# Splitting a projection in two, moving a weighting step and handing a copy from GpSimd to VectorE in a double attention kernel

## Chip, cores and metric

One Trainium2 chip, one core. The metric is the device time of one launch in microseconds (us). The engines are TensorE (PE; its weight loads are shown as PEld), VectorE (DVE), ScalarE (ACT), GpSimd (POOL) and the DMA queues, of which SyncE (SP) issues nearly all.

## What is computed

The layer takes x of 32 batches, 512 tokens and 256 channels, and puts two attentions and one routed feed-forward network behind each other. The feed-forward part is added to batch 0 alone (512 routed rows).

```python
qk = x @ W_attn + b_attn; q, k = qk[..., :C], qk[..., C:]     # 16 heads of 16 channels
y  = causal_attn(q, k, v=x)
e  = x[:, 1:] - y[:, :-1]
k2 = x[:, :-1] @ W_k2 + b_k2
y2 = causal_attn(q[:, 1:], k2, e)
x1 = layernorm(x + proj(y) + proj(y2))        # then layernorm(x1 + ffn(x1))
```

## The kernel before

The work of attention is cut into **units**: one unit is four heads of one attention of one batch, so a batch has 8 units, at **places** 0 to 7 (0 to 3 the first attention, 4 to 7 the second), and the kernel has 256. A unit has ten **slots**. Every engine walks through the same list of times (unit, slot), and does in each slot what is written for it there; within an engine the order is fixed by hand. Semaphores are the only thing that joins the engines. `ahead` is the batch of the present unit.

In each slot TensorE makes one PSUM bank of transposed scores for the present unit (`score_t`, three banks, L682) and one bank of plain scores for the unit five ahead (`score`, three banks, L693), the two next to each other in the upper and lower rows of the array. ScalarE turns each `score_t` bank into probabilities by Exp (L541), GpSimd sets the upper triangle of each pair of banks to zero (L437, slots 1, 3, 5, 7, 9), VectorE takes the row maxima of the `score` banks (L899). The maxima are needed by the unit five ahead: at places 3 and 7, slots 2 and 3, they are transposed (L747), negated and split (L575, L908), and four DMAs of SyncE put them into rows of `stack_q` (L374).

TensorE groups its banks: 0, 1, 2 in slot 0; 3, 4 in slot 3; 5, 6, 7 in slot 5; 8, 9 in slot 8 (`RUNS`). Between them stand, in this order:

- slot 2: `weigh` of the unit before, key blocks 1, 3 and 2 (24 matmuls, L643), which needs all five masks of that unit. ScalarE copies the result to `heads_t` (L567, its slot 2).
- slot 4: the four transposes of `heads_t` (L708). VectorE normalises out of `out_t` behind its own bank 4 (L922, L928).
- slot 7: a **piece** of the projections of the next batch (`PIECES`), six matmuls of 512 columns into the one bank `misc` (L734), at places 7, 0, 1, 2, 4 and 5; at places 3 and 6 instead half of the output projection of the batch before (L776, 8 matmuls for two token blocks j = 0, 1).
- slot 9: `weigh` of the present unit, key block 0 (8 matmuls, L643), which needs the masks of slots 1 and 3 (banks 0 to 3), and VectorE's normalisation of the unit before.

ScalarE reads a piece out of `misc` in slot 7, behind Exp 7 (`part_f`, L553). GpSimd splits it into two parts three slots later, that is in slot 0 of the next unit (`part_h` L457, `part_l` L459), and SyncE issues six DMAs to the stacks in slot 4 (L295).

At places 0 and 1 ScalarE also applies the layer norm of an earlier batch, one quarter each in slots (0,7), (0,9), (1,1) and (1,3) (L276), behind a chain of small operations of GpSimd (`refine`, slot (0,5)) that ends in `shift` (L264). GpSimd adds the bias to `resid` at (3,6) (L445), splits x for the next projections at (6,4) and (6,7) (L469, L471), copies x into `value1` at (5,2) (L483), and in every slot 0 does one 128x256 subtraction or addition (L496, L503).

Of the kernel before, what the change touches and what calls it, by code (L numbers as in the profile page):

```python
# [11 lines left out]
ALU = mybir.AluOpType  # L12
# [3 lines left out]
HEADS, HEAD_DIM = 16, 16  # L16
GROUP = 4
GROUPS = HEADS // GROUP
UNITS = 2 * GROUPS
# [26 lines left out]
TRIANGLES = [(512, 2, 1), (512, 2, 1), (512, 2, 2), (512, 2, 2), (256, 4, 1)]  # L46


PIECES = {(7, 7): ("k", 0, 0), (0, 7): ("q", 0, 1), (1, 7): ("k", 1, 2), (2, 7): ("q", 1, 3),
          (4, 7): ("k2", 0, 4), (5, 7): ("k2", 1, 5)}  # L50
N_PIECES = len(PIECES)
RING, KEY_DEPTH, MAX_DEPTH, JUNK = 6, 3, 3, 2

# [16 lines left out]
def build_layer(nc, x, x_turned, w_attn, b_qk, w_k2, w_proj, b_proj,  # L70
                router_indices, routing_weights, w_up, b_up, w_down, b_down, out):
    batches, tokens, width = x.shape
    blocks = tokens // P
    halves = width // P
# [11 lines left out]
    with ctx:  # L86
# [232 lines left out]
        def _(e):  # L319
# [5 lines left out]
            for time in times:  # L325
# [28 lines left out]
                    e.dma_start(resid[:, :, :], x[b].rearrange("(t p) c -> p t c", p=P)).then_inc(s_resid, 16)  # L354


                ended = time - 7
                piece = piece_ending(ended // SLOTS % UNITS, ended % SLOTS, ended // SLOTS // UNITS, batches)
                if piece and not (piece[0] == "q" and piece[2] == 0):
                    stack_piece(e, *piece)  # L360
# [48 lines left out]
        def _(e):  # L409
# [17 lines left out]
            for time in times:  # L427
# [9 lines left out]
                    e.affine_select(out=view, in_=view, compare_op=ALU.is_ge, fill=0.0, base=-unit_parts(unit)[1],  # L437
                                    pattern=[[0, runs], [0, cut], [1, P]], channel_multiplier=-1).then_inc(s_mask, 1)

                if (place, slot) == (3, 6) and 0 <= ahead - 1 < batches:  # L440
                    wide = bass.AP(bias2[:, :].tensor, bias2[:, :].offset, [list(bias2[:, :].ap[0]), [0, blocks], [1, width]])
                    if ahead == 1:
                        e.wait_ge(s_bias, 1)
                    e.wait_ge(s_resid, 16 * ahead)
                    e.tensor_tensor(resid[:, :, :], resid[:, :, :], wide, ALU.add).then_inc(s_biased, 1)  # L445
# [16 lines left out]
                for c in range(halves):  # L462
                    b = ahead + 2
                    if (place, slot) == (6, (4, 7)[c]) and 0 <= b < batches:
                        if c == 0:
                            e.wait_ge(s_xt, 16 * (b + 1))
                            if b:
# [2 lines left out]
                        e.wait_ge(s_xsplit, 2 * (halves * b + c) + 1)  # L470
                        e.tensor_tensor(x_t[LOW][:, c, :], x_full[:, c, :], x_t[HIGH][:, c, :].bitcast(F32),  # L471
                                        ALU.subtract).then_inc(s_xsplit, 1)


                if (place, slot) == (5, 2) and 0 <= ahead + 1 < batches:
                    b = ahead + 1
                    if b == 0:
                        e.wait_ge(s_wproj, 32)
                        e.tensor_tensor(bias2[:, :], bias2[:, :], bias2[:, :], ALU.add).then_inc(s_bias, 1)
                    e.wait_ge(s_x, 16 * (b + 1))  # L480
                    if b:
                        e.wait_ge(s_pv, GROUP * (UNITS * (b - 1) + GROUPS))
                    e.tensor_copy(value1[:, :, :, 0:HEAD_DIM],  # L483
                                  x_in[:, :, :].rearrange("p t (h d) -> p t h d", d=HEAD_DIM)).then_inc(s_value1, 1)


                done = unit - 2
# [37 lines left out]
        def _(e):  # L525
# [4 lines left out]
            for time in times:  # L530
# [21 lines left out]
                        e.wait_ge(s_split, 2 * (n - 1))  # L552
                    e.activation(part_f[n % 2][:, :], misc[:, :], ACT.Identity, bias=bias_qk[:, column:column + 1]).then_inc(s_full, 1)  # L553

                ended = time - 7
                piece = piece_ending(ended // SLOTS % UNITS, ended % SLOTS, ended // SLOTS // UNITS, batches)
                if piece and piece[0] == "q" and piece[2] == 0:
                    stack_piece(e, *piece)
# [70 lines left out]
        def _(e):  # L629
# [17 lines left out]
            for time in times:  # L647
# [61 lines left out]
                    done.then_inc(s_turned, 1)  # L709


                piece = piece_ending(place, slot, ahead, batches)
                if piece:
                    kind, hf, b, n = piece
                    if n == 0:
                        e.wait_ge(s_wsplit, 2)
                    if kind == "k2" and b == 0:
                        e.wait_ge(s_wsplit, 4)
                    if n:
                        e.wait_ge(s_full, n)  # L720
                    if place == 1 and ahead >= 1:
                        e.wait_ge(s_yt, halves * ahead - 1)
                    if place == 2 and ahead >= 1:
                        e.wait_ge(s_yt, halves * ahead)
                    if place == 4 and ahead >= 1:
                        e.wait_ge(s_attended, 2 * ahead - 1)
                    if place == 7 and ahead + 1 >= 0:
                        e.wait_ge(s_negl, 2 * ahead + 3)
                    for c in range(halves):
                        if n % N_PIECES == 0:  # L730
                            e.wait_ge(s_xsplit, 2 * (halves * b + c + 1))
                        for i, (pw, px) in enumerate(zip(PARTS_K, PARTS_Q)):
                            w = wk2[pw][:, c, hf, :] if kind == "k2" else wq[pw][:, c, hf + (0 if kind == "q" else halves), :]
                            done = e.matmul(misc[:, :], w, x_t[px][:, c, :], start=(c == 0 and i == 0),  # L734
                                            stop=(c == halves - 1 and i == TERMS - 1))
                    done.then_inc(s_piece, 1)
# [14 lines left out]
                if 0 <= b < batches:  # L751
                    for hf in range(halves):
                        if (place, slot) == ((1, 4), (2, 4))[hf]:
                            e.wait_ge(s_full, min(N_PIECES * (b + 2) + 2 + hf, N_PIECES * batches))
                            if hf == 0:
                                e.wait_ge(s_added, GROUPS * (b + 1))
                            else:
                                e.wait_ge(s_yt, halves * b + 1)
                            for t in range(blocks):
                                done = e.transpose(misc[:, t * P:(t + 1) * P], y_sum[b % 2][:, t, hf * P:(hf + 1) * P], ident[:, :])  # L760
                            done.then_inc(s_yt_pe, 1)
                    for pair in range(2):
                        for j in range(2):
                            if (place, slot) == ((3, 6)[pair], 7):
                                t = 2 * pair + j
                                if j == 0:
                                    if b == 0:
                                        e.wait_ge(s_wproj, 32)
                                    e.wait_ge(s_yt, halves * (b + 1))
                                    e.wait_ge(s_full, min(N_PIECES * (b + 2) + (6 if pair else 4), N_PIECES * batches))  # L770
                                    if pair:
                                        e.wait_ge(s_attended, 2 * b + 1)
                                    elif ahead < batches:
                                        e.wait_ge(s_negl, 2 * ahead + 2)
                                for c in range(halves):
                                    done = e.matmul(misc[:, j * width:(j + 1) * width], y_t[:, c, t * P:(t + 1) * P], wp[:, c, :],  # L776
                                                    start=(c == 0), stop=(c == halves - 1))
                                if j:
                                    done.then_inc(s_proj, 1)


                if slot == 9 and 0 <= unit < end:
                    b, a, g = unit_parts(unit)
                    if a:
                        e.wait_ge(s_value2, GROUPS * b + g + 1)
# [70 lines left out]
        def _(e):  # L856
# [27 lines left out]
            for time in times:  # L884
# [3 lines left out]
                if 0 <= unit + LEAD < end:  # L888
                    b, a, g = unit_parts(unit + LEAD)
                    number = time + SLOTS * LEAD  # L890
                    for i, (h, qb, col) in enumerate(MAX_BANKS[slot]):
# [5 lines left out]
                        if count >= JUNK:  # L897
                            e.wait_ge(s_max, count - JUNK + 1)
                        e.tensor_tensor_reduce(junk[count % JUNK][:, 0:n], score[number % MAX_DEPTH][:, col:col + n], mask, 1.0, -3e38,  # L899
                                               ALU.add, ALU.max, max_cols[b % 2][:, a, head % SIDES, head // SIDES, qb:qb + 1]).then_inc(s_max, 1)  # L900

                for a, b in ((0, ahead + 1), (1, ahead)):
                    if (place, slot) == ((7, 3), (3, 3))[a] and 0 <= b < batches:
# [142 lines left out]
```

## Time and profile before

| | |
|---|---|
| runs | 2417.51, 2409.24, 2413.22 us; median 2413.22 |
| profiled execution | 2417.51 us, its span 2415.4 us |
| TensorE busy in the span | 2319.0 us, 96% |
| VectorE busy | 2089.4 us, 87% |
| ScalarE busy | 1778.4 us, 74% |
| GpSimd busy | 1523.3 us, 63% |

The span is the time from the first to the last recorded instruction. The busy time of TensorE has modelled ends, so it also holds short stretches in which the array waits behind the last columns of a matmul; starts of instructions are the better measure there.

### The profile page before, as it was taken

Reading aid. Unit: us, or ns where it says so; the run is one execution under the profiler, and the core shown is the slowest. Engines: PE = TensorE matmul, PEld = TensorE weight load, DVE = VectorE, ACT = ScalarE, POOL = GpSimd, SP = SyncE. Lnnn points to the kernel's source line nnn. Section 1 sums busy time; section 2 is a strip of 40 time slices with the busy share of each in tenths; the row PEclk is TensorE's granted clock in tenths of the full one; section 3 lists DMA queues with packets and bytes.
Section 4 is the critical chain, followed back from the end, with each engine's and each line's share of the span. In section 5 each row is a group of like instructions: output and inputs, shape, how many; then the busy total and the mean of one; then the engine's idle time right before and its main releaser. Section 6 shows DMA issues by size and latency. Waiting matters only on the chain.

```text
span 2415.4 us, 64954 instructions
## 1 busy us (share of the span) xinstructions
PE 2319.0 (96%) x19670; PEld 1327.7 (55%) x19670; DVE 2089.4 (87%) x9242; ACT 1778.4 (74%) x3392; POOL 1523.3 (63%) x2375
## 2 busy tenths in 40 slices
PE   6999999999999999999999999999999999999996
PEld 4555555555555555555555555555555555555454
DVE  5889998899899989999899889999998899998554
ACT  3677777777777777777777777777777777777642
POOL 4466666766766666666666666666666667665432
PEclk7799999999999999999999999999999999999997
DMA  7465555655556556565555665655556555554121
GB/s 122 90 109 105 103 99 98 118 113 112 115 104 112 97 103 123 111 114 112 103 107 101 108 118 111 118 111 108 104 95 117 112 113 117 110 97 81 55 70 35
DMA packets 187732, 250.82 MB, mean 104 GB/s; under 512 B 26744, under 2 KB 103168, under 8 KB 187392
## 3 DMA queue, kind: packets, MB, share of 16 engines
q1 hardware_dynamic: 186432, 245.10, 53.6%
q8 instruction: 166, 2.72, 0.5%
q10 hardware_dynamic: 960, 1.57, 0.5%
q14 instruction: 174, 1.43, 0.3%
HBM read 74.60 MB, written 16.78 MB: 38 GB/s over the span
## 4 chain that ended last, share of the span: by engine, by line
PE 72%; ACT 12%; issue 6%; POOL 4%; DVE 3%; DMA 2%; SPq 1%; ACTq 0%; DVEq 0%; POOLq 0%
PE out_t L643 22%; PE score_t L682 18%; PE misc L734 11%; PE score L693 7%; ACT heads_t L567 5%; PE out_t L708 4%; PE misc L776 4%; ACT prob L541 4%; PE score L835 2%; DVE junk L899 2%; DMA stack_q<-neg_l 1%; POOL prob L437 1%; ACT resid L276 1%; PE misc L760 1%; SPq L374 1%
## 5 line engine op out<-in xcount | busy, mean ns | idle before, releaser
L899 DVE CUSTOM_DVE_ANT_0 junk<-score,mask_rows 128x384 bf16<-128x384 f32 (+3 forms) x3584 | 1686.6, 515 | 224.8 <-PE score L693 215.8
L541 ACT ACTIVATE prob<-score_t 128x512 f32<-128x512 f32 x2560 | 1368.4, 599 | 276.4 <-PE score_t L682 275.5
L437 POOL TENSOR_SCALAR_AFFINE_SELECT prob<-prob 128x512 f32<-128x512 f32 (+1 forms) x1280 | 710.5, 560 | 729.7 <-ACT prob L541 717.9
L682 PE MATMUL score_t<-stack_q,stack_k 50*128 50x128 f32 (+5 forms) x4096 | 985.2, 359 | 25.8 <-ACT prob L541 7.5
L693 PE MATMUL score<-stack_k,stack_q 48*128 48x512 f32 (+3 forms) x4096 | 982.5, 348 | 2.7 <-DVE max_cols L899 1.1
L682 PEld LDWEIGHTS score_t<-stack_q,stack_k 50*128 50x128 f32 (+1 forms) x4096 | 611.8, 186 | 565.6 <-ACT prob L541 304.1
L643 PE MATMUL out_t<-prob,value 128*17 128x512 f32 (+3 forms) x8192 | 658.0, 439 | 0.0
L693 PEld LDWEIGHTS score<-stack_k,stack_q 48*128 48x128 f32 x4096 | 618.4, 188 | 24.8 <-DVE max_cols L899 9.9
L899 DVE DVE_READ_ACCUMULATOR2_ANT max_cols<- 128x1 f32 x4096 | 339.5, 83 | 0.0
L643 PEld LDWEIGHTS out_t<-prob,value 128*17 128x17 f32 x8192 | 184.7, 97 | 211.1 <-issue 129.6
L459 POOL TENSOR_TENSOR part_l<-part_f,part_h 128x512 fp32r<-128x512 f32 x192 | 245.4, 1278 | 16.3
L567 ACT ACTIVATE heads_t<-out_t,sum_floor 128x512 f32<-128x512 f32 x256 | 176.7, 690 | 90.5 <-PE out_t L643 90.3
L553 ACT ACTIVATE part_f<-misc,bias_qk 128x512 f32<-128x512 f32 x192 | 132.2, 689 | 142.1 <-PE misc L734 142.1
L708 PE MATMUL out_t<-ident,heads_t 128*128 128x128 f32 x1024 | 167.8, 286 | 25.5 <-ACT heads_t L567 11.6
L708 PEld LDWEIGHTS out_t<-ident,heads_t 128*128 128x128 f32 x1024 | 107.6, 141 | 87.1 <-ACT heads_t L567 86.8
L899 DVE CUSTOM_DVE_ANT_0 junk<-score,mask_first 128x128 bf16<-128x128 f32 x512 | 146.2, 286 | 0.0
L457 POOL CAST part_h<-part_f 128x512 fp32r<-128x512 f32 x192 | 117.5, 612 | 44.0 <-ACT part_f L553 41.7
L734 PE MATMUL misc<-x_t_h,wq_h 128*128 128x512 f32 x256 | 118.1, 461 | 17.7 <-DVE wq_l L873 9.8
L776 PE MATMUL misc<-wp,y_t 128*128 128x256 f32 x512 | 128.3, 394 | 0.0
L776 PEld LDWEIGHTS misc<-wp,y_t 128*128 128x128 f32 x512 | 93.3, 191 | 21.1 <-issue 8.9
L734 PE MATMUL misc<-x_t_l,wq_h 128*128 128x512 f32 x256 | 103.7, 405 | 0.0
L734 PE MATMUL misc<-x_t_h,wq_l 128*128 128x512 f32 x256 | 103.7, 405 | 0.0
(99 smaller groups left out, 1703.0 us busy)
## 6 DMA issues: line engine op xcount, KB each, us to landing
stack_k<-part_h SPq DMA_DIRECT2D x512, 128.0 KB, 4.5
stack_k<-part_l SPq DMA_DIRECT2D x256, 128.0 KB, 5.1
stack_q<-part_h SPq DMA_DIRECT2D x248, 128.0 KB, 4.2
x_full<-x_turned SPq DMA_DIRECT2D x32, 512.0 KB, 13.1
x_in<-L_attn_x SPq DMA_DIRECT2D x32, 512.0 KB, 14.5
resid<-L_attn_x SPq DMA_DIRECT2D x32, 512.0 KB, 5.2
stack_q<-part_l SPq DMA_DIRECT2D x124, 128.0 KB, 5.1
layer_out<-resid SPq DMA_DIRECT2D x31, 512.0 KB, 7.6
```

The costliest lines, as they stand in the source:

```text
L437: e.affine_select(out=view, in_=view, compare_op=ALU.is_ge, fill=0.0, base=-unit_parts(unit)[1], pattern=[[0, runs], [0, cut], [1, P]], ch ...
L459: e.tensor_tensor(part_l[i][:, :], part_f[i][:, :], part_h[i][:, :].bitcast(F32), ALU.subtract).then_inc(s_split, 1)
L541: e.activation(prob[pair % RING][:, slot % 2 * 512:slot % 2 * 512 + 512], score_t[time % KEY_DEPTH][:, :], ACT.Exp, scale=1.0 / np.sqrt(HE ...
L553: e.activation(part_f[n % 2][:, :], misc[:, :], ACT.Identity, bias=bias_qk[:, column:column + 1]).then_inc(s_full, 1)
L567: e.activation(heads_t[:, :], out_t[:, :], ACT.Identity, bias=sum_floor[:, 0:1]).then_inc(s_heads, 1)
L643: done = e.matmul(out_t[32 * h:32 * h + HEAD_DIM + 1, first:first + count], value[:, kb, GROUP * g + h, :], prob[pair % RING][:, at:at + c ...
L682: done = e.matmul(score_t[now % KEY_DEPTH][:, col:col + n], keys[rows, pair, kb * P:(kb + 1) * P], stack_q[b % 2][rows, pair, kb * P:token ...
L693: done = e.matmul(score[number % MAX_DEPTH][:, col:col + n], stack_q[b % 2][rows, pair, qb * P:(qb + 1) * P], keys[rows, pair, 0:n], start ...
L708: done = e.transpose(out_t[:, t * P:(t + 1) * P], heads_t[:, t * P:(t + 1) * P], ident[:, :])
L734: done = e.matmul(misc[:, :], w, x_t[px][:, c, :], start=(c == 0 and i == 0), stop=(c == halves - 1 and i == TERMS - 1))
L776: done = e.matmul(misc[:, j * width:(j + 1) * width], y_t[:, c, t * P:(t + 1) * P], wp[:, c, :], start=(c == 0), stop=(c == halves - 1))
L899: e.tensor_tensor_reduce(junk[count % JUNK][:, 0:n], score[number % MAX_DEPTH][:, col:col + n], mask, 1.0, -3e38, ALU.add, ALU.max, max_co ...
```

## The change

It touches five things.

1. A piece is cut in two: the three matmuls of channel half c = 0 stay in slot 7, those of c = 1 go to slot 9. The piece now ends in slot 9, so that `part_f` is read in ScalarE's slot 9 (behind Exp 9), and GpSimd splits it in slot 2 of the next unit. SyncE's DMAs stay in slot 4 of the next unit.
2. The output projection at places 3 and 6 is cut in two as well: block j = 0 in slot 7, j = 1 in slot 9.
3. `weigh` of key block 0 goes from slot 9 to slot 7, behind the first half of a piece or of the projection and ahead of banks 8 and 9.
4. The copy of x into `value1` at (5,2) goes from GpSimd to VectorE, behind its maxima of bank 2.
5. The addition of the bias to `resid` on GpSimd goes from (3,6) to (3,2), where it stands ahead of the split of the piece of place 2.

```diff
-PIECES = {(7, 7): ("k", 0, 0), (0, 7): ("q", 0, 1), (1, 7): ("k", 1, 2), (2, 7): ("q", 1, 3),
-          (4, 7): ("k2", 0, 4), (5, 7): ("k2", 1, 5)}
+PIECES = {(7, 9): ("k", 0, 0), (0, 9): ("q", 0, 1), (1, 9): ("k", 1, 2), (2, 9): ("q", 1, 3),
+          (4, 9): ("k2", 0, 4), (5, 9): ("k2", 1, 5)}
...
-                ended = time - 7
+                ended = time - 5
...
-                if (place, slot) == (3, 6) and 0 <= ahead - 1 < batches:
+                if (place, slot) == (3, 2) and 0 <= ahead - 1 < batches:
...
-                if (place, slot) == (5, 2) and 0 <= ahead + 1 < batches:     # on GpSimd
...
-                    e.tensor_copy(value1[:, :, :, 0:HEAD_DIM],
-                                  x_in[:, :, :].rearrange("p t (h d) -> p t h d", d=HEAD_DIM)).then_inc(s_value1, 1)
...
-                piece = piece_ending(place, slot, ahead, batches)
-                if piece:
+                for c in range(halves):
+                    piece = piece_ending(place, slot + 2 * (1 - c), ahead, batches)
+                    if piece:
...
-                            if (place, slot) == ((3, 6)[pair], 7):
+                            if (place, slot) == ((3, 6)[pair], (7, 9)[j]):
...
-                if slot == 9 and 0 <= unit < end:
+                if slot == 7 and 0 <= unit < end:
...
+                if (place, slot) == (5, 2) and 0 <= ahead + 1 < batches:     # on VectorE, behind its maxima
...
+                    e.tensor_copy(value1[:, :, :, 0:HEAD_DIM],
+                                  x_in[:, :, :].rearrange("p t (h d) -> p t h d", d=HEAD_DIM)).then_inc(s_value1, 1)
```

## Rows read from the trace of the kernel before

**Rows 1.** The page, part 1: span; busy time, share and instructions of each engine.

```profile
span 2415.4 us, 64954 instructions
PE 2319.0 (96%) x19670; PEld 1327.7 (55%) x19670; DVE 2089.4 (87%) x9242; ACT 1778.4 (74%) x3392; POOL 1523.3 (63%) x2375
```

**Rows 2.** Windows of units, key-block-0 weighting to weighting: length, busy PE, PEld, DVE, ACT, POOL.

```profile
1001.09:1010.02 8.93, 8.78 (x79) 5.14 (x77) 7.66 (x36) 6.12 (x14) 6.79 (x8) 1.00 0.81 149
...
1018.49:1026.71 8.22, 8.13 (x76) 4.70 (x74) 7.55 (x34) 6.52 (x14) 6.18 (x9) 1.00 0.50 89
...
1052.51:1062.04 9.53, 8.95 (x80) 5.09 (x78) 7.65 (x35) 8.68 (x18) 6.24 (x11) 1.00 0.90 160
...
sum 69.55, PE 68.02 PEld 39.08 DVE 62.95 ACT 53.94 POOL 46.55; mean PE 8.50 PEld 4.89 DVE 7.87 ACT 6.74 POOL 5.82
```

**Rows 3.** Timeline of TensorE, a unit at place 5: start us, length us, instruction.

```profile
1019.47 0.50 PE L682 MATMUL score_t<-stack_q,stack_k 52*128 52x512 f32 x1
...
1020.43 1.49 PE L643 MATMUL out_t<-prob,value 128*17 128x384 f32 x24
...
1022.73 0.66 PE L708 MATMUL out_t<-ident,heads_t 128*128 128x128 f32 x4
...
1024.40 0.50 PE L734 MATMUL misc<-x_t_h,wk_h 128*128 128x512 f32 x1
...
1025.66 0.40 PE L734 MATMUL misc<-x_t_l,wk_h 128*128 128x512 f32 x1
1025.99 0.38 PE L682 MATMUL score_t<-stack_q,stack_k 52*128 52x256 f32 x1
...
1026.71 1.05 PE L643 MATMUL out_t<-prob,value 128*17 128x512 f32 x8
1027.69 0.50 PE L682 MATMUL score_t<-stack_q,stack_k 52*128 52x512 f32 x1
```

**Rows 4.** Timeline of TensorE, a unit at place 3: bank 0, output projection, bank 8.

```profile
1002.08 0.50 PE L682 MATMUL score_t<-stack_q,stack_k 50*128 50x512 f32 x1
...
1007.43 1.99 PE L776 MATMUL misc<-wp,y_t 128*128 128x256 f32 x8
1009.35 0.38 PE L682 MATMUL score_t<-stack_q,stack_k 50*128 50x256 f32 x1
```

**Rows 5.** Timeline of GpSimd at place 3, and its copy at place 5.

```profile
1002.89 0.61 POOL L457 CAST part_h<-part_f 128x512 fp32r<-128x512 f32 x1
1003.58 1.27 POOL L459 TENSOR_TENSOR part_l<-part_f,part_h 128x512 fp32r<-128x512 f32 x1
...
1005.50 0.91 POOL L437 TENSOR_SCALAR_AFFINE_SELECT prob<-prob 128x256 f32<-128x256 f32 x2
...
1007.84 2.36 POOL L445 TENSOR_TENSOR resid<-resid,bias 128x1024 f32<-128x1024 f32 x1
...
1023.27 1.05 POOL L483 COPY value<-x_in 128x1024 f32<-128x1024 f32 x1
```

**Rows 6.** Timeline of ScalarE, places 0 and 1; in brackets the idle time before.

```profile
1051.95 0.69 ACT L553 ACTIVATE part_f<-misc,bias_qk 128x512 f32<-128x512 f32 x1 [0.24 <-PE misc L734]
1053.07 0.60 ACT L276 ACTIVATE resid<-resid,shift,rstd 128x256 f32<-128x256 f32 x1 [0.44 <-POOL shift L264]
1053.58 1.06 ACT L541 ACTIVATE prob<-score_t 128x512 f32<-128x512 f32 x2
```

**Rows 7.** Timeline of TensorE, place 1: the transposes of heads_t.

```profile
1057.71 0.66 PE L708 MATMUL out_t<-ident,heads_t 128*128 128x128 f32 x4 [0.37 <-ACT heads_t L567]
```

**Rows 8.** Timeline of VectorE, place 5: maxima of bank 2, bank 3 and the end of bank 4.

```profile
1021.27 0.69 DVE L899 CUSTOM_DVE_ANT_0 junk<-score,mask_rows 128x512 bf16<-128x512 f32 x1
...
1022.42 0.69 DVE L899 CUSTOM_DVE_ANT_0 junk<-score,mask_rows 128x512 bf16<-128x512 f32 x1 [0.45 <-PE score L693]
...
1023.72 0.08 DVE L899 DVE_READ_ACCUMULATOR2_ANT max_cols<- 128x1 f32 x1
```

**Rows 9.** All copies on VectorE of line 871: nanoseconds, start, shapes.

```profile
L871 DVE CAST wq_h<-wq_full x1: 979/979/979, 6.3 to 6.3; 128x1024 fp32r<-128x1024 f32 x1
```

More of the change, by code:

```diff
@@ L472, in _ @@
                                         ALU.subtract).then_inc(s_xsplit, 1)
-                if (place, slot) == (5, 2) and 0 <= ahead + 1 < batches:
[L476 to L482, printed above, removed]
-                    e.tensor_copy(value1[:, :, :, 0:HEAD_DIM],
-                                  x_in[:, :, :].rearrange("p t (h d) -> p t h d", d=HEAD_DIM)).then_inc(s_value1, 1)
                 done = unit - 2
@@ L553, in _ @@
                     e.activation(part_f[n % 2][:, :], misc[:, :], ACT.Identity, bias=bias_qk[:, column:column + 1]).then_inc(s_full, 1)
-                ended = time - 7
+                ended = time - 5
                 piece = piece_ending(ended // SLOTS % UNITS, ended % SLOTS, ended // SLOTS // UNITS, batches)
@@ L709, in _ @@
                     done.then_inc(s_turned, 1)
-                piece = piece_ending(place, slot, ahead, batches)
-                if piece:
[L714 to L729, printed above, removed]
+                for c in range(halves):
+                    piece = piece_ending(place, slot + 2 * (1 - c), ahead, batches)
+                    if piece:
+                        kind, hf, b, n = piece
+                        if c == 0:
+                            if n == 0:
+                                e.wait_ge(s_wsplit, 2)
+                            if kind == "k2" and b == 0:
+                                e.wait_ge(s_wsplit, 4)
+                            if n:
+                                e.wait_ge(s_full, n)
+                            if place == 1 and ahead >= 1:
+                                e.wait_ge(s_yt, halves * ahead - 1)
+                            if place == 2 and ahead >= 1:
+                                e.wait_ge(s_yt, halves * ahead)
+                            if place == 4 and ahead >= 1:
+                                e.wait_ge(s_attended, 2 * ahead - 1)
+                            if place == 7 and ahead + 1 >= 0:
+                                e.wait_ge(s_negl, 2 * ahead + 3)
                         if n % N_PIECES == 0:
@@ L735, in _ @@
                                             stop=(c == halves - 1 and i == TERMS - 1))
-                    done.then_inc(s_piece, 1)
+                        if c == halves - 1:
+                            done.then_inc(s_piece, 1)
                 for a, b in ((0, ahead + 1), (1, ahead)):
@@ L900, in _ @@
                                                ALU.add, ALU.max, max_cols[b % 2][:, a, head % SIDES, head // SIDES, qb:qb + 1]).then_inc(s_max, 1)
+                if (place, slot) == (5, 2) and 0 <= ahead + 1 < batches:
+                    b = ahead + 1
+                    if b == 0:
+                        e.wait_ge(s_wproj, 32)
+                        e.tensor_tensor(bias2[:, :], bias2[:, :], bias2[:, :], ALU.add).then_inc(s_bias, 1)
+                    e.wait_ge(s_x, 16 * (b + 1))
+                    if b:
+                        e.wait_ge(s_pv, GROUP * (UNITS * (b - 1) + GROUPS))
+                    e.tensor_copy(value1[:, :, :, 0:HEAD_DIM],
+                                  x_in[:, :, :].rearrange("p t (h d) -> p t h d", d=HEAD_DIM)).then_inc(s_value1, 1)
                 for a, b in ((0, ahead + 1), (1, ahead)):
```

## The prediction

> **What bounds the kernel now.** I read the busy shares first, then eight stretches of one batch, then the engines' timelines in them. TensorE is busy 96% of the span, VectorE 87%, ScalarE 74%, GpSimd 63% [rows 1]. The eight units of a batch take 69.55 us, in which TensorE is busy 68.02, VectorE 62.95, ScalarE 53.94 and GpSimd 46.55 [rows 2]; a unit at place 5 takes 8.22 us, one at place 1 9.53, and there ScalarE is busy 8.68 of it. So TensorE's queue is the path nearly everywhere, with two exceptions that matter here: the stretch of the layer norm at places 0 and 1, where ScalarE is the path (TensorE's transposes wait 0.37 us for `heads_t` [rows 7]), and places where VectorE works more than usual and holds back a bank.
>
> In the unit at place 5 the reader can take TensorE's order from the starts [rows 3]: bank 0 at 1019.47, `weigh` of blocks 1, 3, 2 from 1020.43, the transposes at 1022.73, the piece from 1024.40, bank 8 at 1025.99, `weigh` of block 0 at 1026.71, the next bank 0 at 1027.69. So a piece takes 1.59 us from its start to bank 8, banks 8 and 9 take 0.72, `weigh` of block 0 takes 0.98.
>
> **Item 1 to 3, TensorE.** Not one matmul is added or removed. What is added is a change of kind: before, slots 7 to 9 hold piece, banks 8 and 9, `weigh`; after, half a piece, `weigh`, banks 8 and 9, half a piece. That is one boundary more per unit, and the same at places 3 and 6 with the projection's blocks. What does a boundary cost? The piece spends 1.26 us from its first to its last start, five steps, so 0.25 each, but the steps inside are shorter than the first and the last: from the last start to bank 8 are 0.33 us [rows 3]. 512 columns at the granted full clock (the last but two columns of [rows 2] are 1.00, which is 2.4 GHz) are 0.213 us, six of them 1.28, so that a piece carries 0.31 us beyond its columns; `weigh` of block 0, four passes of 512 columns for four heads side by side (2048 columns, 0.85 us), carries 0.13. A small part of the 0.31 recurs with each matmul and does not come twice. I put the additional boundary between 0 (a half piece that runs into `weigh` without a gap) and 0.21 us, and take 0.10, nearer to the excess of `weigh`, since the new neighbours both use all rows of the array.
>
> The Trainium skill (TensorEngine Tiling (Array Packing), "Key Properties") says that changing the tiling mode, not merely the tile, drains TensorE. Scores use half the rows, pieces the whole array, `weigh` a column group per head, so by that page every boundary here costs a drain, the new one too. The trace agrees that a boundary has a price: 0.33 us between the last start of the piece and bank 8 where columns alone are 0.213. By the page the term below would be computed with 0.21 in place of 0.10 and be 37 us in place of 18.
>
> Of the eight boundaries of a batch I count 5.5: at place 0 it is hidden, because at place 1 ScalarE is late anyway; at place 5 it goes into the term of the copy; at place 7 VectorE works nearly without a gap and hides about half. 5.5 x 0.10 x 32 batches = **18 us**; from 0 to 5.5 x 0.21 x 32 = 37.
>
> In an ordinary unit the move of `part_f` is hidden. It is read when the second half ends, at bank 0 of the next unit, and takes about 0.6 us of ScalarE, while Exp 0 can't start before bank 0 is done anyway; the three Exps (0.53 each by the pair in [rows 6]) then end before `weigh` does, 2.4 us behind bank 0 (1020.43 plus 1.49 against 1019.47, [rows 3]), and `heads_t` starts when it did. If that cover were gone, 0.1 us a unit would be due.
>
> **ScalarE at places 0 and 1.** Before, ScalarE fills its wait for GpSimd's `shift` with `part_f` (0.69 at 1051.95), then still waits 0.44 us, and starts the first quarter of the norm at 1053.07 [rows 6]. From there on to `heads_t` it has no gap, and TensorE waits for it [rows 7]. After, slot 7 holds no `part_f`: ScalarE waits for `shift` with nothing to do, since its queue is in order, Exps 8 and 9 stand behind it, and `part_f` comes behind Exp 9, in the stretch without a gap. `shift` isn't earlier, for it hangs on the mask of bank 5 and on its own chain. So `heads_t` is late by about the 0.59 us of `part_f` that are not overlapped, and the transposes, banks 5 to 7 and the rest follow. I take 0.55 x 31 = **17 us**; between 0.3 (if TensorE's waits for ScalarE at place 1 have slack that I don't see) and 0.65, so 9 to 20.
>
> **Item 5, GpSimd at place 3.** Before, the split of the piece of place 2 starts at 1002.89, and lasts to 1004.85, ahead of the first mask of the unit; the masks of slots 1 and 3 follow at 1005.50, and the bias (2.36 us) at 1007.84, when nothing urgent is left [rows 5]. After, the order is: mask of slot 1, bias, split, mask of slot 3. With bank 0 as zero (1002.08 [rows 4]): `part_f` and two Exps end at 0.7 + 1.08 = 1.78, the mask (0.91 for two, so 0.42 to 0.45) at 2.2, the bias at 4.55, the split (0.61 + 1.27 and a gap, 1.96) at 6.5, the mask of slot 3 at 6.9. `weigh` of block 0 now stands in slot 7, behind the first half of the projection; the projection starts at 5.35 (at 1007.43, [rows 4]) and half of its 1.92 us to bank 8 (1009.35) puts `weigh` at 6.3. Its heads 2 and 3 need the mask of slot 3, so it stands 0.5 to 0.6 us. The other waits at TensorE grow shorter by it (VectorE catches up ahead of bank 8 and at place 4), so I count 0.35 x 31 = **11 us**; from 0 (the mask is in time) to 1.3 us, if heads 0 and 1 then run alone and the second pair takes the full 0.85 again, so 0 to 40. In the seven other units the mask of slot 3 is due at about 4.5 and `weigh` at 5.7, more than a microsecond of cover. The split moved behind the mask of slot 1 delays SyncE's six DMAs by about 2 us; the stacks are needed by the banks five units ahead, and at least a whole unit (8.2 us) lies between, so this costs nothing; without that cover each microsecond would stand on TensorE's path.
>
> **Item 4, the copy.** On GpSimd it takes 1.05 us [rows 5] in a unit where GpSimd is busy 6.18 of 8.22 [rows 2], and nobody waits for it: removing it gives nothing. On VectorE the trace has no copy of this shape; the nearest is a cast of 128x1024 from SBUF, 0.979 us [rows 9]. It stands behind the maxima of bank 2, which end at 1021.96, where VectorE waits 0.45 us for bank 3 [rows 8]. So bank 3 starts 0.5 us later, bank 4 ends at 1024.3 instead of 1023.80, and bank 7, which reuses bank 4's buffer, had started just behind that time (the piece that follows it started at 1024.40). TensorE loses about 0.5 us, partly where it would have lost to VectorE at the next unit anyway. 0.45 x 32 = **14 us**; 0 if the copy fits in the 0.45, up to 0.6 x 32 = 19.
>
> The Trainium skill (VectorE: DVE Perf Modes, "The perf-mode tier table") gives an fp32 `tensor_copy` from SBUF two elements a cycle. An estimate from that page is 1024/2 cycles at 0.96 GHz, 0.53 us, and a fixed part; the cast of the same size took 0.979, so the trace doesn't bear the full factor out. By the page the copy term would be about 3 us in place of 14. That belongs to the low case of this term.
>
> **Sum.** 18 + 17 + 11 + 14 = 60 us. Made against the profiled execution, 2417.5 + 60 = 2477.5; that execution was 4.3 above the median of the runs, 2413.2, so I expect **2474 us**, 2.5% slower. Low ends alone give 0 + 9 + 0 + 0, that is 2422; high ends 37 + 20 + 40 + 19 = 116, 2529.
>
> **Rivals.**
>
> - *Smoother feeding wins (the other side).* Mechanism: Exps 8 and 9 no longer stand behind `part_f`, so the `score_t` banks come free some 0.6 us sooner, and no stretch between banks holds a full 1.59 us piece next to nothing. Place: banks 1 and 2 of the next unit. For it: ScalarE's `part_f` does stand ahead of Exp 8 in its queue now [rows 6]. Against: in the unit at place 1 `shift` sets the time of Exp 8 before and after, elsewhere TensorE has hardly a gap to win back; and the stretch between banks 7 and 8 grows from 1.59 to about 0.9 + 0.98. It decides if boundaries cost nothing and it is worth more than the 0.55 of place 0. All that TensorE can win are the 69.55 - 68.02 = 1.53 us a batch in which it is idle [rows 2]. Price: with 0.9 of them gained, 29 us, so 2384. Chance 0.10.
> - *Everything is absorbed.* The boundary is free, the copy fits in VectorE's gap, the mask is in time, and the 0.55 at place 1 is recovered by gaps of ScalarE (busy 8.68 of 9.53 at place 1 [rows 2]). 2413 to 2420. For it: the gaps are there. Against: TensorE is busy 68.02 of 69.55, and has next to nothing with which to catch up. Chance 0.10.
> - *GpSimd's block at place 3 is the large term.* The mask of slot 3 is later than worked out (bias and split each start late), `weigh` stands for 1.3 us or more, and ScalarE and VectorE run dry behind it, which are late at place 4 in turn. 2474 - 11 + 40 + the high end of the boundaries, some 2510. For it: 2.36 + 1.96 us are put ahead of a mask that is wanted two slots later. Against: `weigh` can begin with heads 0 and 1. Chance 0.18.
> - *Forecast*, the four terms as above, 2435 to 2500. Chance 0.62.
>
> **Range and chances.** Low end of the range 2418, which leaves out the faster rival and part of the absorbed one; high end 2520, which takes in most of the block at place 3. Runs of this kernel lie within 0.35% of each other, so 0.3%, 7 us, is about what a measurement can tell from no change. Faster 0.11, within it 0.07, slower 0.82 (forecast, block, and the part of absorbed above 2420).
>
> **What would show it.** Right: at place 5 a unit of about 8.3 to 8.4 us without the copy's effect; ScalarE idle for more than a microsecond ahead of the first norm quarter at place 0, `part_f` behind Exp 9, and the transposes of place 1 waiting near 0.9 us; at place 3 GpSimd without a gap from the mask of slot 1 to that of slot 3, and `weigh` of block 0 waiting for L437; the copy at about 1 us on VectorE and bank 7 of place 5 behind it. Wrong: batches of 69.5 us or less; starts of `weigh` that follow the half piece by no more than its columns; a copy of 0.55 us. The most likely error is the size of the boundary, which counts eight times a batch.

## The result and the profile after

The changed kernel takes 2493.7 us (median of 4 runs, 2490.0 to 2496.9) against 2411.2 us before (4 runs): ratio 1.0341, 95% interval 1.0324 to 1.0357, so 82 us or 3.4% slower. The forecast was 2474 with a range of 2418 to 2520: the direction and the range hold, the sum was 20 us short. The profiled execution shows TensorE as busy as before in share, and 62 us longer busy than in [rows 1], with the same 19670 instructions. The page, span and busy times:

```profile
span 2488.8 us, 64954 instructions
PE 2380.8 (96%) x19670; PEld 1308.3 (53%) x19670; DVE 2122.8 (85%) x9275; ACT 1772.9 (71%) x3392; POOL 1506.0 (61%) x2342
```

The windows of units at places 1, 3 and 5, each from `weigh` of block 0 to the next one (the columns are those of [rows 2]; block 0 is now weighted in slot 7, so a window starts ahead of banks 8 and 9 of the unit before):

```profile
1012.40:1022.71 10.31, 9.15 (x79) 5.05 (x78) 8.12 (x37) 8.95 (x19) 6.80 (x15) 1.00 0.82 147
...
1031.58:1040.63 9.05, 8.90 (x77) 4.87 (x76) 7.46 (x34) 6.83 (x14) 6.59 (x8) 1.00 0.78 146
...
1049.65:1058.37 8.72, 8.60 (x76) 4.57 (x75) 8.27 (x36) 6.52 (x13) 5.61 (x9) 1.00 0.22 46
```

Now the terms one by one. First the cut. TensorE's timeline at place 5, which answers to [rows 3]:

```profile
1057.46 0.50 PE L723 MATMUL misc<-x_t_h,wk_h 128*128 128x512 f32 x1
1057.80 0.40 PE L723 MATMUL misc<-x_t_h,wk_l 128*128 128x512 f32 x1
1058.04 0.40 PE L723 MATMUL misc<-x_t_l,wk_h 128*128 128x512 f32 x1
1058.37 1.05 PE L631 MATMUL out_t<-prob,value 128*17 128x512 f32 x8
1059.35 0.38 PE L670 MATMUL score_t<-stack_q,stack_k 52*128 52x256 f32 x1
...
1060.02 0.50 PE L723 MATMUL misc<-x_t_h,wk_h 128*128 128x512 f32 x1
...
1060.92 0.50 PE L670 MATMUL score_t<-stack_q,stack_k 52*128 52x512 f32 x1
```

Read the starts: the first half takes 1058.37 - 1057.46 = 0.91 us, the second 1060.92 - 1060.02 = 0.90. Before, the whole took 1.59. A cut costs 0.22 us, and it makes no difference whether `weigh` or a bank of scores follows. `weigh` takes 0.98 (1058.37 to 1059.35) as before.

Second, ScalarE at places 0 and 1, which answers to [rows 6] (in brackets the idle time before), and below it TensorE's transposes behind it, which answer to [rows 7]:

```profile
1014.51 0.60 ACT L276 ACTIVATE resid<-resid,shift,rstd 128x256 f32<-128x256 f32 x1 [1.36 <-POOL shift L264]
1015.02 1.06 ACT L529 ACTIVATE prob<-score_t 128x512 f32<-128x512 f32 x2
1015.98 0.68 ACT L541 ACTIVATE part_f<-misc,bias_qk 128x512 f32<-128x512 f32 x1
```

```profile
1019.73 0.66 PE L696 MATMUL out_t<-ident,heads_t 128*128 128x128 f32 x4 [0.95 <-ACT heads_t L555]
```

The wait for `shift` is 1.36 us instead of 0.44, `part_f` stands behind it, and the transposes wait 0.95 instead of 0.37. The window at place 1 grew from 9.53 to 10.31.

`shift` itself also comes later, which the prediction did not have. The split of the piece now stands on GpSimd in slot 2 of place 0, ahead of `var_eps`, with which the small operations for `shift` begin. ScalarE waits for `var_eps`, before and after:

```profile
1049.80 0.20 ACT L269 ACTIVATE log_var<-var_eps 128x4 f32<-128x4 f32 x1 [0.31 <-POOL var_eps L510]
```

```profile
1011.25 0.20 ACT L269 ACTIVATE log_var<-var_eps 128x4 f32<-128x4 f32 x1 [0.56 <-POOL var_eps L498]
```

Counted from the transposes of place 0 (1048.57 before, 1009.77 after), the first quarter of the norm starts after 4.74 us instead of 4.50, and the transposes of place 1 another 5.22 us behind it instead of 4.64.

Third, GpSimd at place 3 (answers to [rows 5]), and TensorE's `weigh` there:

```profile
1035.97 0.42 POOL L437 TENSOR_SCALAR_AFFINE_SELECT prob<-prob 128x256 f32<-128x256 f32 x1 [0.28 <-ACT prob L529]
1036.37 2.36 POOL L445 TENSOR_TENSOR resid<-resid,bias 128x1024 f32<-128x1024 f32 x1
1038.68 0.60 POOL L457 CAST part_h<-part_f 128x512 fp32r<-128x512 f32 x1
1039.37 1.27 POOL L459 TENSOR_TENSOR part_l<-part_f,part_h 128x512 fp32r<-128x512 f32 x1
1040.59 1.60 POOL L437 TENSOR_SCALAR_AFFINE_SELECT prob<-prob 128x256 f32<-128x256 f32 x3
```

```profile
1039.57 1.13 PE L766 MATMUL misc<-wp,y_t 128*128 128x256 f32 x4
1040.63 1.47 PE L631 MATMUL out_t<-prob,value 128*17 128x512 f32 x8
1042.03 0.39 PE L670 MATMUL score_t<-stack_q,stack_k 50*128 50x256 f32 x1
```

GpSimd has no gap from the mask of slot 1 to that of slot 3, which starts at 1040.59. `weigh` begins at 1040.63 with heads 0 and 1 and reaches bank 8 after 1.40 us instead of 0.98.

Fourth, VectorE at place 5 (answers to [rows 8]), and all copies of that line (nanoseconds: least, median, most):

```profile
1054.60 0.97 DVE L900 COPY value<-x_in 128x1024 f32<-128x1024 f32 x1
1055.49 0.68 DVE L889 CUSTOM_DVE_ANT_0 junk<-score,mask_rows 128x512 bf16<-128x512 f32 x1
...
1056.79 0.08 DVE L889 DVE_READ_ACCUMULATOR2_ANT max_cols<- 128x1 f32 x1
1056.79 0.25 DVE L923 RECIPROCAL rden<-out_t 128x16 f32<-128x16 f32 x1
```

```profile
L900 DVE COPY value<-x_in x32: 687/964/969, 49.1 to 2281.5; 128x1024 f32<-128x1024 f32 x32
```

Bank 3's maxima follow the copy with no wait at all, where VectorE waited 0.45 us before, and bank 4 ends at 1056.79 + 0.08 = 1056.87. TensorE's bank 7, which reuses bank 4's buffer, starts behind that; the row of before and the row of after:

```profile
1023.97 0.28 PE L682 MATMUL score_t<-stack_q,stack_k 52*128 52x128 f32 x1
```

```profile
1057.01 0.29 PE L670 MATMUL score_t<-stack_q,stack_k 52*128 52x128 f32 x1
```

Counted from bank 0 (1019.47 and 1052.20), bank 7 starts 4.81 us into the unit instead of 4.50.

### The profile page after: what moved, and what is told of

The parts are those of the page before. It is cut to its first block, busy times and chain, and to the rows that moved or that the text cites. A ratio compares the mean times of both kernels' runs of the same rounds, so it can differ in the third digit from the quotient of the medians.

```text
span 2488.8 us, 64954 instructions
## 1 busy us (share of the span) xinstructions
PE 2380.8 (96%) x19670; PEld 1308.3 (53%) x19670; DVE 2122.8 (85%) x9275; ACT 1772.9 (71%) x3392; POOL 1506.0 (61%) x2342
## 4 chain that ended last, share of the span: by engine, by line
PE 74%; ACT 11%; issue 6%; POOL 4%; DVE 3%; DMA 1%; ACTq 0%; SPq 0%; DVEq 0%; POOLq 0%
PE out_t L631 22%; PE score_t L670 19%; PE misc L723 12%; PE score L681 7%; PE misc L766 5%; ACT heads_t L555 5%; PE out_t L696 5%; ACT prob L529 4%; DVE junk L889 2%; PE score L825 1%; POOL prob L437 1%; PE misc L750 1%; ACT part_f L541 1%; PE score L841 1%; ACT resid L276 1%
## 5 line engine op out<-in xcount | busy, mean ns | idle before, releaser
L631 PE MATMUL out_t<-prob,value 128*17 128x512 f32 (+3 forms) x8192 | 668.1, 437 | 1.0 <-POOL prob L437 0.7
L459 POOL TENSOR_TENSOR part_l<-part_f,part_h 128x512 fp32r<-128x512 f32 x192 | 254.3, 1325 | 16.2
L723 PE MATMUL misc<-x_t_h,wq_h 128*128 128x512 f32 x256 | 131.3, 513 | 17.7 <-DVE wq_l L863 9.8
L766 PE MATMUL misc<-wp,y_t 128*128 128x256 f32 x512 | 144.5, 405 | 0.0
L276 ACT ACTIVATE resid<-resid,shift,rstd 128x256 f32<-128x256 f32 x124 | 75.7, 614 | 41.3 <-POOL shift L264 41.3
```

The lines of the kernel that those rows point to most:

```text
L459: e.tensor_tensor(part_l[i][:, :], part_f[i][:, :], part_h[i][:, :].bitcast(F32), ALU.subtract).then_inc(s_split, 1)
L631: done = e.matmul(out_t[32 * h:32 * h + HEAD_DIM + 1, first:first + count], value[:, kb, GROUP * g + h, :], prob[pair % RING][:, at:at + c ...
```

## Experiments

The theory: four separate losses, namely a price per cut of TensorE's stream, `part_f` behind `shift`, the late mask at place 3, and the copy. The rivals: that one item carries it all, `weigh` ahead of banks 8 and 9 above all, because it leaves ScalarE and VectorE without a bank; or that the losses are hidden by other waits.

**Items 1 to 3 alone.** The changed kernel with

```diff
-                if (place, slot) == (3, 2) and 0 <= ahead - 1 < batches:    # bias
+                if (place, slot) == (3, 6) and 0 <= ahead - 1 < batches:
```

and the copy block back on GpSimd. Expected:

> The changed kernel with the bias back at (3,6) and the value1 copy back on GpSimd: items 1 to 3 alone. Theory A (a boundary of 0.20 us per unit, hidden at one of eight, and part_f pushed behind shift at place 0, 0.57 us a batch): 7 x 0.20 + 0.57 = 1.97 us a batch, less some that VectorE's gate hides, so 55 to 63 us above the kernel before, ratio 1.023 to 1.026. Theory B (the copy and the bias carry most of the 82 us): under 40 us above.

Measured: 2471.4 us, before 2409.1 in the same comparison, 62.3 above, ratio 1.0259 (1.0240 to 1.0278). B falls: the cut pieces and the moved weighting are three quarters of the loss. Theory A's sum holds, but its parts don't. The table gives the mean time in us from the transposes of `heads_t` of one place to those of the next, in 24 batches from the middle of each trace; the third row is the run with one more cut, further down.

| from place | 0 | 1 | 2 | 3 | 4 | 5 | 6 | 7 |
|---|---|---|---|---|---|---|---|---|
| before | 9.14 | 8.59 | 8.68 | 9.02 | 8.26 | 8.42 | 8.58 | 8.78 |
| items 1 to 3 | 10.02 | 8.87 | 8.95 | 9.00 | 8.58 | 8.50 | 8.71 | 8.83 |
| one more cut | 9.99 | 9.07 | 9.15 | 9.00 | 8.77 | 8.68 | 8.72 | 9.02 |

Theory A counted 0.57 us at place 0 and 0.20 at each of seven others. The traces have 0.88 at place 0, 0.28 to 0.32 at places 1, 2 and 4, 0.05 to 0.13 at places 5, 6 and 7, and nothing at place 3: 1.99 us a batch, against the 1.97 of the theory. That the sum fits so well is luck.

**Items 1 and 2 alone**, the weighting back in slot 9:

```diff
-                if slot == 7 and 0 <= unit < end:
+                if slot == 9 and 0 <= unit < end:
```

> Items 1 and 2 alone: pieces and projections split over slots 7 and 9, the weighting of block 0 still in slot 9, behind the second half. Theory A: the boundary comes from the split, whatever stands between the halves, and part_f still ends in slot 9: the same 55 to 63 us above before as items 1 to 3 together. Theory C (the cost is the weighting put ahead of banks 8 and 9, which leaves ScalarE and VectorE without a bank for 1.9 us): at most 20 us above.

Measured: 2542.7 us, ratio 1.0553 (1.0533 to 1.0573), 134 above before. Both theories miss it: this is twice what items 1 to 3 cost together. TensorE's timeline shows why, here a unit at place 5: half a piece, bank 8, bank 9.

```profile
1005.47 0.51 PE L735 MATMUL misc<-x_t_h,wk_h 128*128 128x512 f32 x1
...
1006.37 0.38 PE L682 MATMUL score_t<-stack_q,stack_k 52*128 52x256 f32 x1
...
1007.35 0.35 PE L682 MATMUL score_t<-stack_q,stack_k 52*128 52x256 f32 x1 [0.47 <-DVE max_cols L901]
```

Only the half piece of 0.90 us lies between banks 7 and 8. VectorE hasn't cleared bank 6, whose buffer bank 9 needs, and TensorE stands 0.47 us. Later, behind the second half and the whole weighting, VectorE in turn waits for its next bank:

```profile
1010.22 0.69 DVE L901 CUSTOM_DVE_ANT_0 junk<-score,mask_rows 128x512 bf16<-128x512 f32 x1 [0.91 <-PE score L693]
```

**Item 3 alone**, in the kernel before:

```diff
-                if slot == 9 and 0 <= unit < end:
+                if slot == 7 and 0 <= unit < end:
```

> Item 3 alone: the whole piece in slot 7 and the weighting of block 0 right behind it, then banks 8, 9, 0, 1, 2 in a row. Theory A: one boundary fewer than before (banks 9 and 0 now stand together), 8 x 0.20 = 1.6 us a batch less, of which VectorE, with five banks in a row and three buffers, takes back up to 0.3 us a unit: 10 to 50 us faster than before. Theory C: TensorE works 2.6 us without a bank in each unit, ScalarE and VectorE run dry, 30 us or more slower than before.

Measured: 2606.0 us, ratio 1.0813 (1.0793 to 1.0833), 197 above before. Theory A had it faster and is plainly wrong on this kernel; C is right. The chain is the same as above, only stronger. VectorE waits 1.40 us behind piece and weighting, and then holds TensorE back at bank 1 in the run of five banks, while bank 2 waits for an Exp; VectorE's row, and TensorE's for bank 1 and bank 2:

```profile
1004.95 0.43 DVE L899 CUSTOM_DVE_ANT_0 junk<-score,mask_rows 128x256 bf16<-128x256 f32 x1 [1.40 <-PE score L693]
```

```profile
1005.87 0.47 PE L682 MATMUL score_t<-stack_q,stack_k 50*128 50x512 f32 x1 [0.52 <-DVE max_cols L899]
1006.57 0.47 PE L682 MATMUL score_t<-stack_q,stack_k 50*128 50x512 f32 x1 [0.19 <-ACT prob L541]
```

So the two items can't be added: 134 and 197 alone, 62 together. How much of this is the distance between banks can be read from TensorE's waits for VectorE ahead of a bank (us in all, times, longest; 400 to 2200 us of the span). In order: before, items 1 to 3, items 1 and 2, item 3.

```profile
PE score_t L682 <- DVE max_cols L899: 0.9, 3, 0.5
```

```profile
PE score_t L682 <- DVE max_cols L901: 0.2, 1, 0.2
```

```profile
PE score_t L682 <- DVE max_cols L901: 34.3, 104, 0.5
```

```profile
PE score_t L682 <- DVE max_cols L899: 101.0, 212, 0.5
```

Each item by itself upsets the distance between banks, and together they restore it. The waits for an Exp ahead of a bank are 4.5, 5.0, 3.6 and 32.5 us in the same order. Scaled from 1800 us to the whole kernel, and less what they are before, these two waits make some 186 of the 197 us of item 3 alone. For items 1 and 2 they make 46 of the 71 us by which the run lies above items 1 to 3; the other 25 weren't taken apart.

**One more cut.** Items 1 to 3, with the third matmul of each first half put behind the weighting:

```diff
                         for i, (pw, px) in enumerate(zip(PARTS_K, PARTS_Q)):
+                            if c == 0 and i == 2 and 0 <= unit < end:
+                                continue
...
                     weigh(unit, 0, 0, tokens, start=True)
+                    piece = piece_ending(place, slot + 2, ahead, batches)
+                    if piece:
+                        kind, hf, b, n = piece
+                        w = wk2[HIGH][:, 0, hf, :] if kind == "k2" else wq[HIGH][:, 0, hf + (0 if kind == "q" else halves), :]
+                        e.matmul(misc[:, :], w, x_t[LOW][:, 0, :], start=False, stop=False)
```

> Items 1 to 3 with one more cut: of the three matmuls of a first half, two stay ahead of the weighting in slot 7 and the third goes behind it, ahead of bank 8. Same matmuls, same distance between banks but for the cut itself. Theory A (each cut costs 0.20 us of TensorE): 6 pieces x 0.20 = 1.2 us a batch, less what VectorE hides at one or two places, so 28 to 38 us slower than items 1 to 3 (2471), 2499 to 2509. Rival (the second cut costs less, since piece and weighting both use all rows; what the split costs is mostly the shift of banks 8 and 9): under 15 us.

Measured: 2501.5 us, ratio 1.0367 (1.0342 to 1.0391), 30 above items 1 to 3, as theory A says. The two were timed in different comparisons; by the ratios 1.0367 and 1.0259 it is 26, just under theory A's 28. TensorE's starts: two matmuls, weighting, one matmul, bank 8.

```profile
1008.39 0.51 PE L737 MATMUL misc<-x_t_h,wq_h 128*128 128x512 f32 x1
...
1009.05 1.05 PE L643 MATMUL out_t<-prob,value 128*17 128x512 f32 x8
1010.04 0.49 PE L799 MATMUL misc<-x_t_l,wq_h 128*128 128x512 f32 x1
1010.46 0.38 PE L682 MATMUL score_t<-stack_q,stack_k 52*128 52x256 f32 x1
```

0.66 and 0.42 make 1.08 for three matmuls that took 0.90 uncut: 0.18 us for a cut between neighbours that both use all rows. The rival, a cheap cut there, falls. The table above shows the same for all batches: 0.18 to 0.20 us more from each place with a piece, nothing from places 3 and 6, which have none, and nothing from place 0, where ScalarE is the path.

**Late quarters.** To take `shift` out of ScalarE's way, in the kernel before and in items 1 to 3:

```diff
-APPLY_AT = ((0, 7), (0, 9), (1, 1), (1, 3))
+APPLY_AT = ((0, 9), (1, 3), (1, 5), (1, 7))
```

> The kernel before with the four quarters of the norm moved from (0,7), (0,9), (1,1), (1,3) to (0,9), (1,3), (1,5), (1,7). Theory A (ScalarE is the path from shift to heads_t of place 1): Exp 8 no longer waits for shift, two quarters (1.0 us) leave the stretch, the unit at place 1 goes from 9.54 to about 8.7 us: 20 to 30 us faster. Rival: the later store and load of resid hold SyncE's queue and with it the stacks, no gain or a loss.

> Items 1 to 3 with the norm moved in the same way. Theory A (of their 62 us, 0.57 us a batch are part_f behind shift at places 0 and 1): the unit at place 1 goes from 10.3 to about 8.9 us, 40 to 48 us faster than items 1 to 3 (2423 to 2431), so the distance to the kernel before with late quarters is 40 to 48 us, 15 to 20 less than the 62. Rival (the loss at place 1 is the boundary and VectorE, not ScalarE): the distance stays at about 62 us.

Measured: before with late quarters 2392.1 us, ratio 0.9927 (0.9912 to 0.9943), 17 faster; items 1 to 3 with late quarters 2435.4, ratio 1.0104 (1.0089 to 1.0118). The distance between the two is 43.3 us, against 62.3 without late quarters: 19 us of the change's loss go with the norm at places 0 and 1. This is a difference of two differences, so a few us uncertain. The gain of 17 is less than the 20 to 30 expected. By the traces, the way from place 0 to 1 is 0.90 us shorter (0.84 forecast), but from place 1 to 2 it is 0.12 longer and from place 3 to 4, in the mean, 0.32. The reason for the last is in the waits of TensorE (engine and line, what for, us in all, times, longest; 400 to 2200 us of the span). Before, then before with late quarters:

```profile
PE out_t L708 <- ACT heads_t L567: 9.7, 26, 0.4
...
PE score_t L682 <- DMA stack_q<-neg_l: 2.9, 7, 1.1
```

```profile
PE score_t L682 <- DMA stack_q<-neg_l: 10.2, 11, 2.5
```

The wait for `heads_t` is gone, but the row transfers of the maxima come late eleven times. In SyncE's queue the store of `resid` waits for the last quarter (70.0 us in 1800, nothing before), and the load of `resid` at (2,2) for the store, ahead of the transfers of (2,4) and (3,3).

**The load later.** Late quarters, and

```diff
-                if (place, slot) == (2, 2) and 0 <= b < batches:
+                if (place, slot) == (2, 6) and 0 <= b < batches:
```

> Late norm quarters as in before_late (2392), and SyncE's load of resid from (2,2) to (2,6), so that its wait for the store of the batch before no longer stands ahead of the stack transfers of (2,4) and of the row transfers of (3,3). Theory A (late quarters made TensorE wait 10.2 us for those rows, 2.9 before): that wait goes to 3 us or less, 5 to 9 us faster than before_late, 2383 to 2387. Rival: the load now competes with the row transfers themselves, no gain.

Measured: 2384.5 us, ratio 0.9891 (0.9875 to 0.9907): 1.1% faster than before, the fastest kernel of this study with the next one. The same wait:

```profile
PE score_t L682 <- DMA stack_q<-neg_l: 2.6, 5, 0.8
```

**The same with quarters at (0,9), (1,1), (1,3), (1,5).**

> The same load at (2,6), but with the quarters at (0,9), (1,1), (1,3), (1,5). Two quarters instead of one stand between shift and heads_t of place 1. Theory A (ScalarE has 0.35 us of slack there in before_late, a quarter costs 0.49): within 5 us of late_resid, rather slower. Rival: the earlier store lets SyncE on sooner and it is the faster by 5 us or more.

Measured: 2383.5 us, ratio 0.9896 (0.9879 to 0.9913). No difference to the one above; theory A's "rather slower" isn't seen.

**Item 4 alone**, the copy block on VectorE in the kernel before.

> The kernel before with item 4 alone, the value1 copy on VectorE. Theory A: the copy takes 0.97 us, 0.45 of it in VectorE's gap before bank 3, the rest holds back bank 7 of place 5: 0.3 to 0.55 us a batch, 10 to 17 us slower, ratio 1.004 to 1.007. Rival: VectorE catches up within the unit, no difference, ratio within 0.002 of 1.

Measured: 2420.3 us, ratio 1.0044 (1.0025 to 1.0063), 11 us. As theory A says.

**Item 4 undone** in the changed kernel, which leaves the bias at (3,2) as the only addition to items 1 to 3.

> The changed kernel with item 4 undone: items 1 to 3 and the bias at (3,2). It has the bias as the only difference to items 1 to 3 alone, which ran 62 us above the kernel before. Theory A (the bias and the split stand ahead of the mask of slot 3, the weighting at place 3 took 1.40 us instead of 0.98): 0.42 us a batch more, 12 to 14 us, so 74 to 77 us above before, ratio 1.031. Rival: what TensorE loses at place 3 it has back at place 4, 62 to 66 us above.

Measured: 2482.9 us, ratio 1.0303 (1.0290 to 1.0317), 74 above before and 11.5 above items 1 to 3. The changed kernel stands 10.8 above this one (2493.7), the copy's price a second time. The ratios give about 11 and 9, and the trace has 0.43 us a batch more from place 3 to 4, where the bias is (9.43 against 9.00).

**Item 5 alone**, the bias at (3,2) in the kernel before.

> The kernel before with item 5 alone, the bias at (3,2). Theory A: the weighting of block 0 stands in slot 9 here, some 10 us behind bank 0 of place 3, and the split is done before; the mask of slot 3 is in time: ratio within 0.002 of 1. Rival (the long GpSimd operation early in the unit hurts by itself, through the masks or the shared memory access of VectorE): 8 us or more slower.

Measured: 2407.7 us, ratio 0.9996 (0.9984 to 1.0009). Nothing. The 11.5 us come only together with the split and the weighting that the other items put next to it.

**Statistics in VectorE's gap.** Late quarters, and

```diff
-STATS_AT = ((5, 5), (6, 4), (7, 5), (0, 1))
+STATS_AT = ((5, 2), (6, 2), (7, 2), (0, 2))
```

> The kernel before with late norm quarters (2392) and the four bn_stats moved from (5,5), (6,4), (7,5), (0,1) to slot 2 of places 5, 6, 7 and 0, behind the maxima of bank 2, where VectorE waits 0.45 to 0.7 us for bank 3. Theory A (work of VectorE in its gap before bank 3 is free up to the length of the gap, elsewhere it holds back a bank): 0.2 to 0.5 us a batch faster than late quarters alone, 6 to 16 us. Rival (VectorE's position is no matter, only its sum): no difference.

Measured: 2391.8 us, ratio 0.9915 (0.9896 to 0.9933), against 2392.1 and 0.9927. A miss: no difference that can be told. In the traces the way from place 5 to 6 is 0.21 us shorter than with late quarters alone (8.21 against 8.42), and the one from place 4 to 5, whose gap took in the operation, no longer (8.26 against 8.25). That is theory A's effect, once. The way from place 0 to 1 is 0.15 longer (8.39 against 8.24), and takes most of it back; what causes that wasn't tried apart.

## Why the prediction was right, and by how much its terms were off

| Term of the sum | predicted | measured | from |
|---|---|---|---|
| boundary on TensorE | 18 | 43 | items 1 to 3 minus before, both with late quarters |
| `part_f` behind `shift` | 17 | 19 | 62.3 - 43.3 |
| these two, by place | 35 | 34 + 27 | the table of places: 1 to 7, and 0, times 31 |
| mask at place 3 | 11 | 11.5 | item 4 undone minus items 1 to 3 |
| copy on VectorE | 14 | 11 | item 4 alone; 10.8 by undoing it |
| sum (without the third row) | 60 | 85 | whole change: 82 |

- **The boundary** is the mis-sized term. I set it between 0 and 0.21 us and took 0.10, "nearer to the excess of `weigh`". The trace after shows 0.22 for a piece, and the additional cut 0.18. With 0.21 the term would have been 37 and the forecast 2493. The count of 5.5 boundaries came near in sum, with some luck: 43 us over 32 batches and 0.21 us are 6.4 of eight, and places 1 to 7 of the table have 1.11 us a batch, about five cuts. But they aren't where I put them. Place 3 loses nothing, places 5 to 7 together 0.26, and places 1, 2 and 4 more than a cut each; why is open. Place 0 is hidden as I said, but only as long as ScalarE is the path there: with late quarters in both kernels the way from place 0 to 1 still differs by 0.37.
- The rule of the Trainium skill that I set beside the row (TensorEngine Tiling (Array Packing), "Key Properties": a change of tiling mode drains TensorE) has no price, but it pointed to the upper bound of 0.21, the better number. The trace agrees with it as far as a price goes at the changes measured here (a piece to `weigh`, a piece to scores); that it is the mode and not the kind of data was not taken apart.
- **ScalarE at places 0 and 1**: right in place and mechanism, and near in size: the idle time before the first quarter (more than a microsecond forecast, 1.36 seen) and the transposes' wait (0.9 forecast, 0.95 seen). What I missed is the 0.24 us by which `shift` itself is late behind the moved split, some 7 us in all; it is most of why place 0 alone shows 27 us and not 17.
- **GpSimd at place 3**: right, down to `weigh` beginning with heads 0 and 1 and losing 0.42 us. That the other places have cover is borne out by `weigh` of block 0, which takes 0.98 us in the median at each of them and 1.40 at place 3.
- **The copy**: right, with bank 7 behind it (0.31 us a batch, and 11 us over 32 are 0.34). The cast of 0.979 us was the better guide than two elements a cycle, but for a reason that I did not have (below).
- **SyncE's six DMAs 2 us later**: cost nothing, as said; none of TensorE's waits in the trace after is for a transfer of a piece.
- **Smoother feeding**, the rival of the other side, did not occur: at place 5 Exp 8 starts 0.60 us behind the start of bank 8 instead of 0.69, not 0.6 sooner, and no place of the table is shorter by more than 0.02. But I had the feeding of the banks down as something that could only help or do nothing. The waits in the runs with one part alone show that it costs some 46 and 186 us when it goes wrong. That the sum came out near the measurement rests on the fact that items 1 to 3 together keep the distances between banks. I had not worked that out, so this part of the agreement is luck: for item 3 alone, by the same reasoning, I expected a gain.
- **GpSimd's block as the large term**: did not occur. Its price was also added up wrongly: 2474 - 11 + 40 + 19 is 2522, not some 2510.
- **The sum**: 2477.5 less 4.3 is 2473, not 2474.

## What to carry to other kernels

When an engine's stream alternates between kinds of matmul, count the changes of kind as work, with the price that the rows of the kernel show: the last start of a group to the next group's first, and first start to second. When three buffers link two engines that are both near 90% busy, write down the distance between consecutive banks before and after: a move is judged by the longest gap and by the longest run it makes, not by its own cost, and two moves that are each bad may repair one another. In a queue that is kept in order by hand, look at what a waiting instruction holds up: here the quarters of a norm, begun one step too early, cost 17 us (all four were moved), and a load behind a late store another 8.

## What the hardware showed beyond that

The copy of 128x1024 fp32 on VectorE takes 687 ns at 49 us, where GpSimd does nothing, and 964 ns in the median, beside GpSimd's work. GpSimd pays as well: the `part_l` subtraction takes 1.59 us in the 31 cases in which it starts during the copy, and 1.27 in the other 161. VectorE's copy, and GpSimd beside it:

```profile
49.12 0.69 DVE L900 COPY value<-x_in 128x1024 f32<-128x1024 f32 x1
```

```profile
1054.41 0.61 POOL L457 CAST part_h<-part_f 128x512 fp32r<-128x512 f32 x1
1055.11 1.59 POOL L459 TENSOR_TENSOR part_l<-part_f,part_h 128x512 fp32r<-128x512 f32 x1
```

In the run with item 4 alone the copy (1020.51 to 1021.45, 0.94 us) has another neighbour on GpSimd: a subtraction of 128x256 that takes 0.73 us elsewhere.

```profile
1019.62 1.28 POOL L459 TENSOR_TENSOR part_l<-part_f,part_h 128x512 fp32r<-128x512 f32 x1
1020.86 1.18 POOL L493 TENSOR_TENSOR value<-x_next,y_sum 128x256 f32<-128x256 f32 x1
```

So there are four meetings of the copy with GpSimd's work, and in each the instruction that started second takes longer by the overlap less 0.14 us. The copy starts second to the cast (overlap 0.42, 0.28 longer than 0.69) and, in the other run, to `part_l` (0.39, 0.25 longer). It starts first before `part_l` (overlap 0.46, `part_l` 0.32 longer) and before the subtraction (0.59, 0.45 longer). The cast and `part_l` take their usual 0.61 and 1.28 us where they start first. This looks like the second waiting for the first, and not like both running slower; it is read from two runs, and no run varied it alone.

The two elements a cycle of the Trainium skill (VectorE: DVE Perf Modes, "The perf-mode tier table") are there when VectorE is alone. 1024/2 cycles at 0.96 GHz are 0.53 us, an estimate by that page; the row has 0.69, and what the other 0.16 are no run here shows. The Trainium skill's GPSIMD Engine Reference ("1. Specifications") names a contention with VectorE for SBUF interfaces, among other cases when VectorE runs in a 2-port mode; these rows fit it.
